# Routed expert tiles: the transposing DMA turns the gate-times-up product instead of the rows, and TensorE turns the rows

## The reference, cut to what matters

```python
gu = einsum('nh,eih->nei', x_flat, experts_gate_up)   # x_flat: layer-normed rows, h = 256
g, u = gu[..., :352], gu[..., 352:]
h = silu(g) * u
expert_out = einsum('nei,ehi->neh', h, experts_down)  # back to width 256
out = einsum('neh,ne->nh', expert_out, w)             # w: softmax scores of the two experts
```

## Time and profile before

| | us |
|---|---|
| median of three executions | 860.83 (860.33 to 862.62) |
| the profiled execution | 859.56 |
| its span, first to last instruction | 857.3 |
| PE busy in the span | 766.9 (89%) |
| DVE busy | 558.2 (65%) |
| ACT busy | 403.1 (47%) |
| POOL busy | 336.2 (39%) |

### The profile page before, as it was taken

One profiled execution on the slowest core, in us unless ns is written; L12 is line 12 of the kernel. 1 busy time (PEld: TensorE's weight loads), 2 busy tenths in 40 slices (PEclk: granted clock), 3 DMA queues, 4 the chain that ended last, 5 costly groups with the idle time before them and its releaser, 6 DMA issues.

```text
span 857.3 us, 22758 instructions
## 1 busy us (share of the span) xinstructions
PE 766.9 (89%) x8336; PEld 492.6 (57%) x8336; DVE 558.2 (65%) x1174; ACT 403.1 (47%) x679; POOL 336.2 (39%) x498
## 2 busy tenths in 40 slices
PE   3788897978888999998989798999999999999996
PEld 2444453544454555554456455777777777756554
DVE  5666786868888889887656776433333333357777
ACT  3225664546464666666554452444444444433331
POOL 5142334278555555544322350111111111157773
PEclk9979998989999999999999899999999999999999
DMA  4744554546444555545320222333333333333643
GB/s 141 199 131 151 170 164 131 150 137 175 135 142 140 154 127 155 154 128 177 113 73 21 87 99 75 87 85 84 88 87 87 87 85 85 86 100 117 215 142 103
DMA packets 108541, 104.33 MB, mean 122 GB/s; under 512 B 52755, under 2 KB 87827, under 8 KB 108437
## 3 DMA queue, kind: packets, MB, share of 16 engines
q1 hardware_dynamic: 90868, 68.47, 29.5%
q0 software_dynamic: 9552, 26.10, 9.3%
q10 hardware_dynamic: 8016, 8.33, 3.0%
HBM read 52.78 MB, written 38.14 MB: 106 GB/s over the span
## 4 chain that ended last, share of the span: by engine, by line
PE 55%; DVE 19%; issue 6%; ACT 6%; DMA 5%; POOL 4%; SPq 3%; ACTq 1%; DVEq 0%; POOLq 0%
PE ps_st L1776 15%; PE ps_m L1798 8%; PE ps_st L1422 6%; DVE mx L956 5%; PE ps_st L1064 5%; PE ps_m L1138 4%; PE ps_o L1114 4%; DMA arena<-ffn_dram 2%; PE ps_m L1204 2%; PE ps_o L1433 2%; DVE qk L1667 2%; DVE xr L1679 2%; PE ps_st L1082 2%; DVE xr L1652 2%; PE ps_st L1098 1%
## 5 line engine op out<-in xcount | busy, mean ns | idle before, releaser
L956 DVE TENSOR_REDUCE mx<-ps_st 128x4 f32<-128x1024 f32 x128 | 155.6, 1217 | 29.1 <-PE ps_st L1082 21.2
L775 ACT ACTIVATE p<-ps_st 128x1024 f32<-128x1024 f32 x128 | 131.0, 1024 | 76.5 <-PE ps_st L1098 69.1
L1776 PE MATMUL ps_st<-fwh,p 128*128 x568 | 138.5, 313 | 0.0
L1529 POOL DMA_DIRECT2D sorted_out<-p x71 | 38.4, 541 | 199.0 <-ACT p L1579 195.0
L1776 PE MATMUL ps_st<-fwl,p 128*128 x284 | 88.8, 313 | 0.0
L1064 PE MATMUL ps_st<-maskq,identb 64*64 64x512 bf16 x512 | 53.5, 408 | 37.2 <-DVE mx L956 35.2
L1354 POOL DMA_INDIRECT expert_rows<-hrow,slot x64 | 64.8, 1012 | 45.2 <-DVE slot L1345 29.6
L1776 PEld LDWEIGHTS ps_st<-fwh,p 128*128 128x128 f16 x568 | 55.6, 98 | 26.4
L1064 PE MATMUL ps_st<-mb_k,identb 64*64 64x512 bf16 x256 | 52.2, 404 | 13.8 <-ACT p L775 13.0
L1537 POOL DMA_INDIRECT p<-sorted_out,xn x52 | 53.8, 1034 | 23.9 <-issue 12.8
L1422 PE MATMUL ps_st<-q,arena 128*128 128x512 f16 x264 | 59.2, 379 | 2.5 <-DVE qk L1667 2.5
(11 more groups left out here) (240 smaller groups left out, 1843.6 us busy)
## 6 DMA issues: line engine op xcount, KB each, us to landing
arena<-ffn_dram SPq DMA_DIRECT2D x20, 544.0 KB
sorted_out<-p POOLq DMA_DIRECT2D x71, 128.0 KB, 2.0
qk_scratch<-arena SPq DMA_DIRECT2D x32, 256.0 KB, 2.6
qk<-qk_scratch SPq DMA_DIRECT2D x44, 128.0 KB, 2.9
xr<-x_dram SPq DMA_DIRECT2D x8, 512.0 KB, 5.0
arena<-ctx_dram SPq DMA_DIRECT2D x16, 256.0 KB, 3.0
hT_dram<-hT ACTq DMA_DIRECT2D x16, 256.0 KB, 3.3
out_dram<-xr SPq DMA_DIRECT2D x16, 256.0 KB, 3.0
```

What stands on the lines that cost most here:

```text
L775: eng.activation(expo[n % 4][:, :, :], ps_st[pair["T", n]][:, :].rearrange("p (h q) -> p h q", h=4), ACT.Exp, scale=SCALE).then_inc(s_e, 1)
L956: eng.tensor_reduce(mx[b % 2][:, qt, :].rearrange("p (h g j) -> p h g j", h=2, g=HG)[:, :, hg, :], ps_st[pair["S", 8 * b + n]][:, :].rearr ...
L1529: eng.dma_start(sorted_out[k * P:(k + 1) * P, :], ys[k % 3][:, :]).then_inc(r_st[k % 3], 16)
L1776: last = mm(o[:, 0:INTER], xgT[k % NXG][:, xl, dc, :], (fwh, fwl)[wl][:, bass.ds(e, 1), w0 + dc * INTER:w0 + (dc + 1) * INTER], start=dc = ...
```

## The change

The rows of a tile now come by a plain DMA into `xg` (three buffers, rows on partitions). PE turns them (four fp16 transposes, `rows_T`) into PSUM, and DVE copies the result into `xgT` (`transposed`, two buffers). The product is no longer turned on PE: ACT makes its high half in rows (`hr`, columns 0 to 383), DVE its low half (columns 384 to 767), and SP's transposing DMA (`turn`) moves the six 128x128 blocks, SBUF to SBUF, into `hrT` (four buffers). The down projection comes three tiles behind instead of two and alternates between two PSUM banks. The three instruction lists after the change, cut to the routed loop:

```diff
 # SP
-                if k >= NXG:
-                    eng.wait_ge(r_u, k - NXG + 1)
-                eng.dma_start_transpose(xgT[k % NXG]..., expert_rows[bass.ds(at, P), :]).then_inc(r_x[k % NXG], 16)
-            for k in range(NTILE):
-                load(k)
+                if k >= 3:
+                    eng.wait_ge(r_t, k - 2)
+                eng.dma_start(xg[k % 3][:, :], expert_rows[bass.ds(at, P), :]).then_inc(r_x[k % 3], 16)
+            def turn(k):
+                eng.wait_ge(r_hl, k + 1)
+                if k >= NHT:
+                    eng.wait_ge(r_y, k - NHT + 1)
+                eng.dma_start_transpose(hrT[k % NHT]..., hr[k % NHR]).then_inc(r_hx[k % NHT], 16)
+            for k in range(NTILE + AHEAD):          # AHEAD = 2
+                if k < NTILE:
+                    load(k)
+                if k >= AHEAD:
+                    turn(k - AHEAD)
 # DVE
+            def transposed(k):
+                eng.wait_ge(r_t, k + 1)
+                if k >= 2:
+                    eng.wait_ge(r_u, k - 1)
+                eng.tensor_copy(xgT[k % 2]..., half_of(ps_d[0])[:, 0:4 * P]...).then_inc(r_tx, 1)
+            transposed(0)
             for k in range(NTILE + 1):
                 ...                                  # hf of tile k
+                if k + 1 < NTILE:
+                    transposed(k + 1)
                 ...
                 if k:
                     b = k - 1
                     eng.wait_ge(r_hh, b + 1)
-                    eng.tensor_tensor(hl[b % 2]..., ps_d[1 + b % 2]..., hh[b % 2]..., ALU.subtract).then_inc(r_hl, 1)
+                    eng.tensor_tensor(hr[b % NHR][:, NC * P:wide], hf[b % 2][:, 0:NC * P], hr[b % NHR][:, 0:NC * P],
+                                      ALU.subtract).then_inc(r_hl, 1)
 # PE
+            def rows_T(k):
+                eng.wait_ge(r_x[k % 3], 16 * (k // 3 + 1))
+                ...                                  # r_tx of the tile before, or f_acc for the first
+                ...                                  # four transposes of xg[k % 3] into ps_d[0]
+                last.then_inc(r_t, 1)
+            rows_T(0)
-            for k in range(NTILE + 2):
+            for k in range(NTILE + LATER):          # LATER = 3
                 if k < NTILE:
-                    eng.wait_ge(r_x[k % NXG], 16 * (k // NXG + 1))
+                    eng.wait_ge(r_tx, k + 1)
                     ...                              # gate and up
-                ...                                  # three fp32 transposes of tile k-1
+                if k + 1 < NTILE:
+                    rows_T(k + 1)
+                if 0 <= k - LATER < NTILE:
+                    b = k - LATER
+                    eng.wait_ge(r_hx[b % NHT], 16 * (b // NHT + 1))
+                    ...                              # down projection of tile b
 # ACT
-                    eng.activation(hh[(k - 1) % 2]..., ps_d[1 + (k - 1) % 2]..., ACT.Copy).then_inc(r_hh, 1)
+                    eng.activation(hr[b % NHR][:, 0:NC * P], hf[b % 2][:, 0:NC * P], ACT.Copy).then_inc(r_hh, 1)
```

More of the change, by code:

```diff
@@ L1443, in ffn @@
         NGB = 5
-        NXG = 4
+        NHR, NHT, LATER, AHEAD = 3, 4, 3, 2
         carve = moe.carve
@@ L1466, in ffn @@
         halfs = [e.bitcast(FP16) for e in flat_expo]
-        xgT = [halfs[0][:, 2 * D * i:2 * D * (i + 1)].rearrange("p (l c t) -> p l c t", l=2, c=DC) for i in range(NXG)]
+        xg = [halfs[0][:, 2 * D * i:2 * D * (i + 1)] for i in range(3)]
+        xgT = [h.rearrange("p (l c t) -> p l c t", l=2, c=DC) for h in (halfs[0][:, 6 * D:8 * D], halfs[1][:, 0:2 * D])]
         ys = [flat_expo[1][:, D * (i + 1):D * (i + 2)] for i in range(3)]
@@ L1474, in ffn @@
         half_of = lambda ps: ps[:, :].bitcast(FP16)
+        wide = 2 * NC * P
+        hr = [halfs[2][:, 0:wide], halfs[2][:, wide:2 * wide], halfs[3][:, 0:wide]]
+        hrT = [h.rearrange("p (l c t) -> p l c t", l=2, c=NC)
+               for h in (moe.awl[:, 0:wide], moe.awl[:, wide:2 * wide], moe.hl0[:, 0:wide], moe.hl0[:, wide:2 * wide])]
         f_c, f_after = moe.f_c, moe.f_after
@@ L1482, in ffn @@
         f_dch = sem("f_dch")
-        r_x = [sem(f"r_x{i}") for i in range(NXG)]
-        r_g = sem("r_g"); r_u = sem("r_u"); r_si = sem("r_si"); r_hf = sem("r_hf")
-        r_ht = sem("r_ht"); r_hh = sem("r_hh"); r_hl = sem("r_hl"); r_y = sem("r_y"); r_ys = sem("r_ys")
+        r_x = [sem(f"r_x{i}") for i in range(3)]
+        r_hx = [sem(f"r_hx{i}") for i in range(NHT)]
+        r_t = sem("r_t"); r_tx = sem("r_tx"); r_g = sem("r_g"); r_u = sem("r_u"); r_si = sem("r_si"); r_hf = sem("r_hf")
+        r_hh = sem("r_hh"); r_hl = sem("r_hl"); r_y = sem("r_y"); r_ys = sem("r_ys")
         r_pad = sem("r_pad")
@@ L1506, in load @@
                 at = eng.value_load(rowmap[0:1, k:k + 1], min_val=0, max_val=XROWS - P)
-                if k >= NXG:
-                    eng.wait_ge(r_u, k - NXG + 1)
-                eng.dma_start_transpose(xgT[k % NXG].rearrange("p l c t -> p (l c) t"),
-                                        expert_rows[bass.ds(at, P), :]).then_inc(r_x[k % NXG], 16)
-            for k in range(NTILE):
-                load(k)
+                if k >= 3:
[5 more added lines that the diff above has]
+                    eng.wait_ge(r_y, k - NHT + 1)
+                eng.dma_start_transpose(hrT[k % NHT].rearrange("p l c t -> p (l c) t"), hr[k % NHR])\
+                    .then_inc(r_hx[k % NHT], 16)
+            for k in range(NTILE + AHEAD):
[3 more added lines that the diff above has]
+                    turn(k - AHEAD)
             eng.wait_ge(moe.s_tw, 16 * NB)
@@ L1566, in _ @@
                 if 0 <= k - 1 < NTILE:
[L1567 to L1579, removed]
+                    b = k - 1
+                    eng.wait_ge(r_hf, b + 1)
+                    if b >= NHR:
+                        eng.wait_ge(r_hx[(b - NHR) % NHT], 16 * ((b - NHR) // NHT + 1))
+                    eng.activation(hr[b % NHR][:, 0:NC * P], hf[b % 2][:, 0:NC * P], ACT.Copy).then_inc(r_hh, 1)
+                if 0 <= k - LATER < NTILE:
+                    b = k - LATER
+                    eng.wait_ge(r_y, b + 1)
+                    if b >= 3:
+                        eng.wait_ge(r_st[b % 3], 16 * (b // 3))
+                    eng.activation(ys[b % 3][:, :], ps_d[2 + b % 2][:, 0:D], ACT.Copy).then_inc(r_ys, 1)
             for n in range(BEFORE, len(STEPS)):
@@ L1694, in _ @@
             eng.wait_ge(r_pad, 2)
+            def transposed(k):
+                eng.wait_ge(r_t, k + 1)
+                if k >= 2:
+                    eng.wait_ge(r_u, k - 1)
+                eng.tensor_copy(xgT[k % 2][:, :, :, :],
+                                half_of(ps_d[0])[:, 0:4 * P].rearrange("p (l c t) -> p l c t", l=2, c=DC)).then_inc(r_tx, 1)
+            transposed(0)
             for k in range(NTILE + 1):
@@ L1700, in _ @@
                     if k >= 2:
[L1701 removed]
+                        eng.wait_ge(r_hl, k - 1)
                     eng.tensor_tensor(hf[k % 2][:, 0:INTER], ps_u[k % 2][:, 0:INTER], gs[k % 2][:, 0:INTER],
                                       ALU.mult).then_inc(r_hf, 1)
+                if k + 1 < NTILE:
+                    transposed(k + 1)
                 if k % 4 == 3:
@@ L1761, in _ @@
             expert = [None]
+            def rows_T(k):
+                eng.wait_ge(r_x[k % 3], 16 * (k // 3 + 1))
+                if k:
+                    eng.wait_ge(r_tx, k)
+                else:
+                    eng.wait_ge(f_acc, 2 * BEFORE)
+                for part in range(2):
+                    for dc in range(DC):
+                        at = part * DC + dc
+                        last = eng.transpose(half_of(ps_d[0])[:, at * P:(at + 1) * P],
+                                             xg[k % 3][:, at * P:(at + 1) * P], identh[:, :])
+                last.then_inc(r_t, 1)
             eng.wait_ge(f_emap, 1)
             experts = {}
-            for k in range(NTILE + 2):
+            rows_T(0)
+            for k in range(NTILE + LATER):
                 if k < NTILE:
                     experts[k] = e = eng.value_load(emap[0:1, k:k + 1], min_val=0, max_val=NE - 1)
-                    eng.wait_ge(r_x[k % NXG], 16 * (k // NXG + 1))
+                    eng.wait_ge(r_tx, k + 1)
                     for w0, o, s_out in ((0, ps_g[k % 2], r_g), (UP0, ps_u[k % 2], r_u)):
@@ L1775, in _ @@
                             for wl, xl in TERMS:
-                                last = mm(o[:, 0:INTER], xgT[k % NXG][:, xl, dc, :],
+                                last = mm(o[:, 0:INTER], xgT[k % 2][:, xl, dc, :],
                                           (fwh, fwl)[wl][:, bass.ds(e, 1), w0 + dc * INTER:w0 + (dc + 1) * INTER],
@@ L1779, in _ @@
                         last.then_inc(s_out, 1)
-                if 0 <= k - 1 < NTILE:
-                    b = k - 1
-                    eng.wait_ge(r_hf, b + 1)
-                    if b >= 2:
[L1784 to L1793, removed]
```

(15 more changed lines are left out.)

3 lines of the change are left out of this document (removed).

## The result

Four executions of the changed kernel gave a median of 1064.85 us (1062.6 to 1070.45), four of the kernel before, on the same chip, 860.58 (859.84 to 862.62): a ratio of 1.238 [1.233, 1.243]. The forecast was 1087 in a range of 995 to 1175. The profiled execution took 1062.6, its span 1060.8, where the working had 1085. The experiments further down ran on several chips, on which the kernel before itself took 859 to 897 us; each ratio is against the kernel before on the same chip.

The account below looks back on a forecast made before the run. PE bounded the routed stage at 3.10 us a tile; after the change, terms summing to a 6.31 us round trip, 68 times, with start and tail, end the stage 226 us later: 1087 us, range 995 to 1175.

Parts of the forecast that it names:

- 1 low half: Routed stage, DVE: the low half, 128x384, takes 0.56 us of each tile's round trip.
- 2 hand-over to SP: Routed stage, from DVE's low half to SP: 0.10 us, taken for each hand-over.
- 6, 7 rows_T to the copy's start: Routed stage: four fp16 transposes on PE, 0.39 us, then the hand-over to DVE, 0.10.
- One sign: Routed stage: PE was to be about half busy, 3.0 of 6.3 us a tile.
- Term 3: SP's issue of the six-block turn: 1.62 us, 0.33 fixed and the rest growing with the blocks.
- Term 4: SP's register load for the row offset, in front of every load: 0.75 us.
- Term 7: Hand-over to DVE, 0.10 us, and its 128x512 copy out of PSUM, 0.69 by the nearest fp32 row.
- Term 5: Landing of a plain row load of 128 KB in the routed stage: 2.0 us.
- the cheap turn: Rival: SP's SBUF-to-SBUF turn issues in 0.33 us like a plain issue; round trip 5.02, total 999; chance 0.08.
- The slow clock: Rival: PE's clock stays at 0.50, rows_T takes up to 0.39 us more a tile; total 1114; chance 0.11.
- Both rivals with the loads in time: Routed loads come in time: PE stays the bound, 854 us, chance 0.03; or DVE is late, 879, chance 0.03.
- What covers the rest: Routed stage: turn's landing has two more tiles (12 us), PE and DVE idle half the time, POOL's result writes stay behind.

Follow-up runs that it names:

- e1: Changed kernel with SP's loads three tiles ahead instead of two (AHEAD 3); 911.75 us, ratio 1.033 to the kernel before.
- e4: Changed kernel with the turn moving only the high half, three blocks instead of six; 1071.05 us, ratio 1.214 to the kernel before.
- e2: Changed kernel with the next tile's row offset read into its register before SP's turn; 1049.3 us, ratio 1.190 to the kernel before.
- e5: Changed kernel with AHEAD 4 instead of 2, so two loads are ahead; 877.35 us, ratio 1.020 to the kernel before.
- e12: Changed kernel, AHEAD 4, rows turned between gate and up, head filled, early expert number, loads on POOL, down projection four tiles behind; 886.13 us, ratio 0.988.
- e7: Changed kernel with AHEAD 4, next tile's rows turned between gate and up, and head and tail filled; 869.37 us, ratio 1.012 to the kernel before.

## Why the prediction was right, point by point

The mechanism is the one forecast, with its place and its sign: e1 shows it. The terms, from copy end to copy end, forecast against the mean of the trace of after:

| term | forecast | measured |
|---|---|---|
| 1 low half | 0.56 | 0.50 |
| 2 hand-over to SP | 0.10 | 0.03 |
| 3 issue of the turn | 1.62 | 1.30 |
| 4 register load | 0.75 | 1.11 |
| 5 landing of the rows | 2.00 | 2.15 |
| 6 hand-over to PE | 0.10 | 0.05 |
| 6, 7 rows_T to the copy's start | 0.49 | 0.47 |
| 7 copy | 0.69 | 0.42 |
| sum (of unrounded terms) | 6.31 | 6.02 |

The low half's own duration is 0.549; it starts 0.05 before the copy ends. The difference in the time comes from the terms: 68 x (6.31 - 6.02) = 20 of the 22 us between 1085 and 1062.6. The other 2 to 3 are the net of two parts: copy 2 ended 4.5 earlier than forecast (533.76 against 538.28), 3.6 of which lie ahead of the stage in this execution (first row load at 518.67, against 522.29), while the tail was 1.0 and what follows 0.7 longer. One sign came out otherwise: PE was to be about half busy and is busy in 264 of 400 us: matmuls are shown longer than their starts are apart, and the granted clock was 0.88, not 1.00.

- Term 3 was mis-sized by its rule (part of the issue in proportion to the blocks). e4 shows the issue to be the same for three blocks as for six, within 0.03; the 1.19 of rows 5, unscaled, would have been nearer than 1.62. The mean of 1.30 lies above the median of 1.24 because of single ones up to 2.11.
- Term 4 was too low. It was read off gaps behind a transpose out of DRAM, beside which the word's read takes 0.27; behind the turn out of SBUF the read alone takes 0.34 more (0.61), and 0.75 + 0.34 = 1.09 is about the 1.11 measured. e2 and e4 show that it is the turn that slows it; why a source in SBUF does and one in DRAM doesn't is not shown. Terms 3 and 4 together are 2.41, forecast 2.37: the sum is right with both parts wrong.
- Term 7: the copy takes 0.425, not the 0.69 of the fp32 row on line 1015. That row was one of another width of data and of another operation, with two inputs. The Trainium skill, VectorE: DVE Perf Modes, section "The perf-mode tier table", had given an estimate of 0.39 and with it a total of 1067; here it agrees, and the row did not.
- Term 5 lies between the row writes of the same stage and the loads of the attention stage, as taken.

The rivals: the cheap turn is refuted by an issue of at least 1.21 on every one of the 71 turns. For the Trainium skill's sentence that initiating a DMA is usually small beside it (DMA: Bandwidth & Descriptors, section "Issuing engines are not separate DMA queues") this form is an exception: 1.24 of a landing of 3.3. The slow clock came in part: the granted clock was 0.88 in the stage, against 1.00 before, and from the first transpose of rows_T to the copy it takes 0.47 on average where it is 0.43 at clock 1.00, 0.04 a tile of the 0.39 that the rival would have put there. That 0.39 was too much as well: where the granted clock was 0.50, the lower level, it takes 0.65, 0.21 more. Both rivals with the loads in time needed another tie between the lists; e5 to e12 give it by hand, and three further waits (PE's register load, the turned product, the tail) turned out to stand hidden behind the rows. With the first taken away the kernel was at 1.005, not at the 0.99 that 854 would have been. Only e12, with the second taken away too, came to 0.988, on its one chip, and the stage's share of that is 1 us.

What covers the rest held: the turned product was late for two tiles only, both behind the last gate and up, 2.8 us together.

## What to carry to other kernels

When a step moves into a queue that works in order, write its list out with what each entry waits for, and follow one entry back to itself: if load(j+1) stands behind something that needs load(j), each tile pays a full round trip, however many buffers there are, and busy times alone don't tell it. Then count the small instructions of the new list too, since a register read behind a DMA of another kind may cost twice as much. And a gain of 0.10 a tile comes only as far as the waits hidden behind the bound are covered too: three were found here, and the distance came to 3.015 when the two inside the stage were covered (e12).

## What the runs showed of the hardware

- The issue of a transposing DMA holds SP's queue for 1.21 us with three blocks out of SBUF, 1.19 with four out of DRAM and 1.24 with six out of SBUF: over three to six blocks it hardly depends on the size. Its landing does grow, 2.8 and 3.3 us with three and six.
- A read of one word from SBUF into a register takes SP 0.27 us behind a transpose out of DRAM, 0.36 behind one of three blocks out of SBUF and 0.61 behind one of six; on PE's queue it takes 0.30 in the kernel before and 0.53 in e7. The Trainium skill, DMA: Bandwidth & Descriptors, section "Latency and other measured facts", gives some 600 ns as the floor of a `tensor_load`. The trace calls these reads TENSOR_LOAD and does not agree: 0.61 is the value behind the turn of six blocks, and the least is 0.26.
- The DMA share of the stage went from 0.33 in the changed kernel to 0.67 in e7, at nearly twice the pace, and the landing of the plain row loads only from 2.0 to 2.1 us in the median (2.15 to 2.32 in the mean).
